# Nested Strassen for the second product of the query and key stage, in 12 groups of two heads

## The reference, cut to what matters

```
x1 = einsum('bct,bcd->bdt', x, cond_weights[idx])       # mixing of the channels, 64 x 32 x 512
q, k, v = x1 @ Wq + bq, x1 @ Wk + bk, x1 @ Wv + bv      # 2048 tokens x 512 -> 4096 (32 heads x 128)
q, k = rms_norm(q, gq), rms_norm(k, gk)                 # over all 4096 columns
out = softmax(q @ k.T / sqrt(128)) @ v                  # per head, 32 tokens of a batch with each other
x = x + out @ Wo + bo
x = x + ffn(x @ w_eff.T)                                # w_eff: weight quantised with a codebook, plus LoRA
```

## Time and profile before

| | |
|---|---|
| median of 3 runs | 1451.27 us |
| the profiled execution | 1450.27 us, of which the span of the trace 1448.4 us |
| PE busy | 1443.8 us (100% of the span) |
| DVE busy | 1079.1 us (75%) |
| POOL busy | 746.3 us (52%) |
| ACT busy | 726.7 us (50%) |
| granted clock of PE | 1.00 |

### The profile page before, as it was taken

How to read it: one execution, slowest core, us unless ns; L and a number is a source line. 1 busy time by engine, 2 the same in 40 slices (tenths; PEclk the granted TensorE clock), 3 DMA queues, 4 the chain that set the end, 5 groups by cost and what they waited for, 6 DMA issues and landing times.

```text
span 1448.4 us, 34721 instructions
## 1 busy us (share of the span) xinstructions
PE 1443.8 (100%) x14507; PEld 1200.6 (83%) x14507; DVE 1079.1 (75%) x1507; ACT 726.7 (50%) x1331; POOL 746.3 (52%) x530
## 2 busy tenths in 40 slices
PE   9999999999999999999999999999999999999999
PEld 8788888888888888888888888888888888888887
DVE  8788868687786777875478888867987667667663
ACT  7766676766766667676333333334432322222221
POOL 7668777777777877776345555514561111112100
PEclk9999999999999999999999999999999999999999
DMA  4211011110111011102443343447653334244230
GB/s 152 66 45 45 31 38 45 45 44 25 45 45 45 29 39 45 45 31 67 138 155 137 131 136 134 145 151 244 200 195 110 103 118 132 85 136 132 74 118 30
DMA packets 106989, 135.13 MB, mean 93 GB/s; under 512 B 6224, under 2 KB 89424, under 8 KB 106320
## 3 DMA queue, kind: packets, MB, share of 16 engines
q1 hardware_dynamic: 105968, 132.49, 27.7%
q10 hardware_dynamic: 864, 0.42, 0.1%
HBM read 86.75 MB, written 46.14 MB: 92 GB/s over the span
## 4 chain that ended last, share of the span: by engine, by line
PE 97%; DVE 1%; ACT 1%; DMA 0%; issue 0%; SPq 0%; DVEq 0%
PE bank L717 42%; PE bank L960 25%; PE bank L736 21%; PE bank L919 4%; PE bank L845 3%; PE bank L988 1%; PE bank L1006 1%; DMA qk<-in_x_nat 0%; PE bank L666 0%; DVE qreg L1708 0%; PE bank L1017 0%; PE bank L974 0%; ACT xs_hi L1160 0%; DVE wa L1624 0%; DVE sqst L1708 0%
## 5 line engine op out<-in xcount | busy, mean ns | idle before, releaser
L717 PE MATMUL bank<-xs_hi,wa 128*128 128x512 f32 x1792 | 563.3, 392 | 0.1
L1527 POOL TENSOR_TENSOR accr<-accr,sqst 128x512 f32<-128x512 f32 x248 | 353.2, 1435 | 147.7 <-ACT sqst L1197 107.5
L717 PEld LDWEIGHTS bank<-xs_hi,wa 128*128 128x128 f32 x1792 | 336.3, 188 | 74.1 <-DVE qk L1775 2.3
L717 PE MATMUL bank<-xs_lo,wa 128*128 128x512 f32 x896 | 348.7, 389 | 0.0
L960 PE MATMUL bank<-ot,wo_main 128*128 128x512 f32 x1344 | 316.4, 392 | 0.0
L960 PEld LDWEIGHTS bank<-ot,wo_main 128*128 128x128 f32 x1344 | 249.5, 188 | 52.6
L736 PE MATMUL bank<-wv,xs_hi 128*128 128x512 f32 (+1 forms) x1008 | 282.6, 366 | 0.1
L1624 DVE TENSOR_TENSOR wa<-wraw,wa 128x256 fp32r<-128x256 f32 (+1 forms) x160 | 157.0, 982 | 96.7 <-ACT wa L1106 95.0
L1322 ACT ACTIVATE ot<-bank,vec 128x256 fp32r<-128x256 f32 x256 | 100.3, 476 | 239.0 <-PE bank L960 146.6
L736 PEld LDWEIGHTS bank<-wv,xs_hi 128*128 128x128 f32 x1008 | 182.1, 189 | 32.9 <-issue 1.9
L717 PEld LDWEIGHTS bank<-xs_lo,wa 128*128 128x128 f32 x896 | 168.3, 188 | 33.2
(11 more groups left out here) (224 smaller groups left out, 1726.9 us busy)
## 6 DMA issues: line engine op xcount, KB each, us to landing
values_b<-v_spill SPq DMA_DIRECT2D x60, 512.0 KB, 4.9
wraw<-in_wqk SPq DMA_DIRECT2D x32, 512.0 KB, 3.5
v_spill<-qk SPq DMA_DIRECT2D x64, 256.0 KB, 2.3
v_spill<-sqst SPq DMA_DIRECT2D x64, 256.0 KB, 2.2
score_spill<-sqst SPq DMA_DIRECT2D x32, 256.0 KB, 2.0
wraw<-in_wv SPq DMA_DIRECT2D x16, 512.0 KB, 5.1
wraw<-score_spill SPq DMA_DIRECT2D x16, 512.0 KB, 4.0
spare<-in_wo SPq DMA_DIRECT2D x15, 512.0 KB, 4.8
```

The lines of the kernel that those rows point to most:

```text
L717: ins = pe.matmul(dst[:, :], wa[:, col:col + P], xpart[:, j - 1, kt, n * CH:(n + 1) * CH], start=(first and k == 0), stop=(k == 5), skip_g ...
L1527: pool.tensor_tensor(a, a, sq_slot(count), ALU.add).then_inc(acc_done, 1)
```

## The change

Second product p2 has a weight block (256 x 128) by a token block (256 x 512) for each head and half. In 12 groups of two heads (steps 12 to 59, `NEST`), the p2 of four steps are taken together as one 256 x 256 by 256 x 1024 product, and it is done by seven sub-products of Strassen-Winograd, each of one 128x128 block and 3 matmuls. These are 21 matmuls for four steps instead of 24. In a step with s % 4 = 3 PE does sub-products 1 and 2 of the next group in the place where p2(s+1) stood, then 6 and 5 (s % 4 = 0), 3 and 7 (s % 4 = 1), and 4 alone (s % 4 = 2). The other steps keep p2.

What comes with it:

- ACT copies sub-products 1, 6, 5 and 7 out of their bank (`nest_keep`), two to `rqk` in SBUF and two to bank 7, and makes the high parts x, y, z (256 columns each) and a (128); the split 1 has 256 columns instead of 512 in these steps.
- DVE makes the low parts of them, and `block_11` has two instructions in steps with s % 4 = 0 and 3, and one more, `start_11`, with s % 4 = 1. In steps 1 and 2 of a group `block_11(s)` stands in step s, not in s-1 (`late_q`), and its square and gain on ACT behind `keep_a1`.
- POOL makes the four sums of the sub-weights (`add_nest`, 128 columns each) in steps with s % 4 = 2, and once the token operands (`nest_operands`, 12 instructions in steps 4 to 10).
- The second level of the quantiser in a step moves from s % 6 = 1 to s % 4 = 0 (steps 12 to 44, nine as before).
- Bank 7 no longer takes scores; all heads' scores go to bank 3.
- SP loads 256 more columns for each group (`load_side`), saves two token blocks and the update once to HBM, and brings them back at the end.

```diff
-    return 0 if s < 6 or s > 59 else 2 if s > 6 and s % 6 == 1 else 1
+    return 0 if s < 6 or s > 59 else 2 if 12 <= s <= 44 and s % 4 == 0 else 1
...
+            def nest(s, m):
+
+                k = nest_no(s)
+                if m == 1:
+                    pe.wait_ge(nest_lo["x"], k + 1)
+                    pe.wait_ge(c11_done, s)
+                elif m == 6:
...
+                    pe.wait_ge(nest_lo["y"], k + 1)
+                    pe.wait_ge(nest_kept[1], k + 1)
+                elif m == 5:
+                    pe.wait_ge(c11_done, s + 1)
+                elif m == 3:
+                    pe.wait_ge(nest_lo["z"], k + 1)
+                    pe.wait_ge(nest_kept[5], k + 1)
+                elif m == 7:
+                    pe.wait_ge(nest_kept[6], k + 1)
+                elif m == 4:
+                    pe.wait_ge(nest_lo["a"], k + 1)
+                    pe.wait_ge(nest_kept[7], k + 1)
+                dst = bank[2 if m in (1, 6, 7, 4) else 6]
+                for i, (w_lo_part, x_lo_part) in enumerate(((0, 0), (0, 1), (1, 0))):
+                    ins = pe.matmul(dst[:, :], nest_w(m, w_lo_part), nest_x(m, x_lo_part),
+                                    start=(m in (1, 2, 5) and i == 0), stop=(i == 2), skip_group_check=True)
...
-                p2(s + 1)
+                if not nested(s + 1):
+                    p2(s + 1)
+                elif s % 4 == 3:
+                    nest(s + 1, 1)
+                    nest(s + 1, 2)
+                elif s % 4 == 0:
+                    nest(s, 6)
+                    nest(s, 5)
+                elif s % 4 == 1:
+                    nest(s - 1, 3)
+                    nest(s - 1, 7)
+                else:
+                    nest(s - 2, 4)
```

ACT's order, from `keep_a1` of a step on:

```diff
+                if late_q(s):
+                    k_upper(s)
+                    if s % 2 == 0:
+                        split_qk(1, h + 1)
                 keep_a1(s + 1)
...
+                if late_q(s):
+                    first_q(s)
+                else:
+                    k_upper(s)
+                    if s % 2 == 0 and s >= 2 and h + 1 < H:
+                        split_qk(1, h + 1)
+                if nested(s + 2) and s % 4 == 2:
+                    nest_split(s + 2, "x")
+                if nested(s + 1) and s % 4 == 3:
+                    nest_keep(s + 1, 1)
+                if nested(s) and s % 4 == 0:
+                    nest_keep(s, 6)
+                    nest_keep(s, 5)
+                if nested(s) and s % 4 == 1:
+                    nest_keep(s - 1, 7)
                 act.wait_ge(p_done[4], s + 1)
...
+                if nested(s) and s % 4 == 0:
+                    nest_split(s, "z")
+                    nest_split(s, "a")
+                if nested(s + 2) and s % 4 == 2:
+                    nest_split(s + 2, "y")
```

DVE's:

```diff
                 if s >= 2:
                     block_12(s - 1)
+                if nested(s) and s % 4 == 1:
+                    start_11(s)
...
+                if late_q(s):
+                    block_11(s)
                 if s % 2 == 1 and h + 1 < H:
                     low_qk(7, h + 1)
-                if s + 1 < N_QK:
+                if s + 1 < N_QK and not late_q(s + 1):
                     block_11(s + 1)
...
                 elif h + 1 < H:
                     low_qk(1, h + 1)
+                    if nested(s + 2) and s % 4 == 2:
+                        nest_low(s + 2, "x")
+                        nest_low(s + 2, "y")
+                    if nested(s) and s % 4 == 0:
+                        nest_low(s, "z")
+                        nest_low(s, "a")
```

and in `block_11` itself, for s % 4 = 3:

```diff
+                        dve.wait_ge(nest_kept[5], k + 1)
+                        dve.wait_ge(nest_kept[7], k + 1)
+                        link(dve.tensor_tensor(dst, bank[7][:, :], a1, ALU.add))
+                        dve.tensor_tensor(dst, dst, rqk[:, :], ALU.add).then_inc(c11_done, 1)
```

More of the change, by code:

```diff
@@ L74, with nested, late_q, nest_no @@
           4: WV_SQST + 2048, 3: WV_ACCR + 3584}
+NEST = range(3, 15)
+def nested(s):
+    return NEST[0] <= s // 4 <= NEST[-1] and s < N_QK
+def late_q(s):
+    return nested(s) and s % 4 in (1, 2)
+def nest_no(s):
+    return s // 4 - NEST[0]
 def wa_cols(j, h):
@@ L352, in build @@
         gq_hi = sem("gq_hi")
+        nest_done = {m: sem(f"n{m}_done") for m in (1, 5, 6, 7)}
+        nest_kept = {m: sem(f"n{m}_kept") for m in (1, 5, 6, 7)}
+        nest_hi = {part: sem(f"n{part}_hi") for part in "xyza"}
+        nest_lo = {part: sem(f"n{part}_lo") for part in "xyza"}
+        nest_added = sem("nest_added")
+        ld_side = sem("ld_side")
+        t_made = sem("t_made")
+        t_made_hi = sem("t_made_hi")
+        t_made_lo = sem("t_made_lo")
+        saved = sem("saved")
+        back = sem("back")
         sq_ready = sem("sq_ready")
@@ L450, in load_raw, with load_side @@
                 sp.wait_ge(s_added[4], h)
+                if nested(2 * h - 2) and h % 2 == 1:
+                    sp.wait_ge(nest_lo["x"], nest_no(2 * h) + 1)
+                    sp.wait_ge(nest_added, 4 * nest_no(2 * h) + 4)
                 sp.dma_start(wraw[:, 0:1024], wqk[h]).then_inc(ld_raw, 16)
+            def load_side(h):
+                k = nest_no(2 * h)
+                if k == 0:
+                    sp.wait_ge(saved, 48)
+                else:
+                    sp.wait_ge(nest_lo["a"], k)
+                    sp.wait_ge(nest_added, 4 * k)
+                sp.dma_start(side, wqk[h + 1][:, 256:512]).then_inc(ld_side, 16)
             load_raw(1)
@@ L485, in _ @@
                     load_raw((s + 3) // 2)
+                if s == 5:
+                    sp.wait_ge(c12_done, 5)
+                    sp.dma_start(up_spill, update[0]).then_inc(saved, 16)
+                    sp.wait_ge(x_act, x_act_at(2, 3))
+                    sp.wait_ge(x_dve, x_dve_at(2, "l3"))
+                    for part in range(2):
+                        sp.dma_start(x12_spill[part], x12[part].bitcast(F32)).then_inc(saved, 16)
+                if s % 4 == 1 and nested(s + 3):
+                    load_side((s + 3) // 2)
+                if s == 4 * NEST[-1] + 2:
+                    sp.wait_ge(p_done[2], s + 2)
+                    for part in range(2):
+                        sp.dma_start(x12[part].bitcast(F32), x12_spill[part]).then_inc(back, 16)
+                    sp.dma_start(update[0], up_spill).then_inc(back, 16)
                 if s == N_QK - 3:
@@ L759, in weights_ahead @@
             def weights_ahead(s, j):
+                if j == 7 and nested(s + 1):
+                    j = 2
+                    s += 1
                 s, j = {6: (s, 5), 5: (s + 1, 1), 1: (s - 1, 7), 7: (s + 1, 2), 2: (s - 1, 4), 4: (s, 3), 3: (s + 1, 6)}[j]
@@ L1257, in _ @@
                     keep_a3(s)
-                act.wait_ge(c11_done, s + 1)
-                square(sq_q_lo(s), 0, s % 2, blk["q_lo", s % 3], None)
-                gain("q_lo", s, gq_lo)
+                if not late_q(s):
+                    first_q(s)
                 h = s // 2
@@ new lines, in t_lo_part, with nest_operands @@
+            def t_lo_part(i, count):
+                pool.wait_ge(t_made_hi, count)
+                pool.tensor_tensor(nest_t(i, 1), spare[:, 2048 + 512 * i:2560 + 512 * i], nest_t(i, 0).bitcast(F32), ALU.subtract)\
+                    .then_inc(t_made_lo, 1)
+            def nest_operands(s):
+                r11, r12, r22, r21 = (spare[:, 512 * i:512 * (i + 1)] for i in range(4))
+                t1, t2 = spare[:, 2048:2560], spare[:, 2560:3072]
+                if s == 4:
+                    whole_x(0)
+                    whole_x(1)
+                elif s == 5:
+                    whole_t(0, r12, r11, 2)
+                    whole_x(2)
+                elif s == 6:
+                    whole_t(1, r22, t1, 4)
+                    whole_t(2, r22, r12, 4)
+                elif s == 7:
+                    whole_x(3)
+                    whole_t(3, r21, t2, 7)
+                elif s == 9:
+                    t_lo_part(1, 1)
+                    t_lo_part(0, 2)
+                elif s == 10:
+                    t_lo_part(2, 3)
+                    t_lo_part(3, 4)
@@ L1845, in _ @@
                 if s == 61:
+                    dve.wait_ge(back, 48)
                     effective(0)
```

162 lines of the change are left out of this document (149 added, 13 removed).

## The result

1510.55 us, the median of four runs (1508.47 to 1511.56), against 1451.24 before: ratio 1.0407, 95% interval 1.0389 to 1.0425. The change makes the kernel 59 us slower. The direction and the place were forecast, the size was not: 1479 was predicted, with 1506 as the end of the range.

The account below looks back on a forecast made before the run. PE was taken as the bound, busy 1443.8 of 1448.4 us. Per group -0.68 + 1.7 + 0.5 + 0.4 + 0.3 = +2.2 us, twelve groups +26.6, once +1, gave 1479 us; forecast range 1462 to 1500, whole range 1449 to 1506.

Parts of the forecast that it names:

- the ceiling of 0.68 us per group: On PE in steps with s % 4 = 2: three matmuls fewer per group save at most 0.68 us, 8.2 in all.
- p4 of B: PE's product p4 in steps with s % 4 = 3: forecast stall 1.5 to 1.8 us per group, 1.7 taken.
- the 6.2 us without POOL: On DVE: earliest start of block_12 for the s % 4 = 2 step, 6.2 us after T, if nothing holds DVE up.
- rivals 1 and 2: Whole kernel: everything hidden, 1443 us, chance 0.07; or DVE free in s % 4 = 2, 1447 to 1451 us, chance 0.20.
- p3 of B: PE's product p3 in steps with s % 4 = 3, waiting for block_22: stall 0 to 0.75 us, 0.5 taken.
- p3 of D: PE's product p3 in steps with s % 4 = 1: stall 0 to 1.1 us, 0.4 taken as mean over 12 groups.
- scores: PE's scores, waiting for a gain behind the next block_12: stall 0 to 0.9 us per group, 0.3 taken.
- The step that failed: On DVE and POOL: one of three low parts waits for POOL's addition, so block_12 starts at 7.4 to 7.7 us.
- T: Time zero of the reckoning: when the product after the scores begins on PE in a step with s % 4 = 2.
- if POOL is two squares behind: Case at the low parts on DVE: each waits a full 1.25 us and the stall at p4 is 3.4 us.
- rival 3: Saturation: POOL and DVE exclude each other and fill their shared time; +4.5 us or more per group, 1505 and up, chance 0.08.
- token operands: 12 POOL instructions in steps 4 to 10, placed in POOL's idle time: 1 us once, at most 6.

Follow-up runs that it names:

- e2: The change with POOL adding only 16 of the 512 columns of each square in steps 10 to 59; 1451.6 us, ratio 1.0001.
- e11: e8 with the 16-column additions of e2; 1447.0 us, ratio 0.9975.
- e1: The change with DVE's low parts x and y moved one step later, x behind block_12, y behind low part 7; 1495.1 us, ratio 1.0305.
- e7: e6 with block_22 ahead of low part 6 in odd steps of the groups; 1493.3 us, ratio 1.0292.
- e8: e7 with low part 4 behind the next block_12, and low part 1 ahead of the second level in steps with s % 4 = 0; 1480.6 us, ratio 1.0205.
- e6: e1 with low part 1 moved into DVE's idle time ahead of block_11; 1481.4 us, ratio 1.0216.
- e10: e8 with the nine second levels of the quantiser left out; 1470.3 us, ratio 1.0132.
- e3: The change with ten more matmuls on PE behind sub-products 1 and 2, filling the stand before p4; 1506.6 us, ratio 1.0383.

## Why the prediction was wrong in size

Right: the sign; the ceiling of 0.68 us per group (36 matmuls fewer); the place (p4 of B waits for `keep_a3`, that for `last_q`, that for `block_12(A)`, that for low parts 1, x and y held up by POOL); the 6.2 us without POOL (measured 6.15); the length of the way from `block_12(A)` to p4 of B (4.2 us, 4.3 forecast). The times of rivals 1 and 2, everything hidden or nearly so, are neared only by e2 and e11, with most of POOL's additions taken away. The rule of the Trainium skill, *SBUF — State Buffer*, "Who interferes with whom", that the two exclude each other for a whole instruction, is borne out: 1.51 us for 256 columns, of which 0.42 is the instruction.

Wrong, term by term, per group:

| term | forecast | measured |
|---|---|---|
| p4 of B | 1.7 | 2.5 (2.75 between starts less 0.23) in eleven groups, less in the last |
| p3 of B | 0.5 | 0.2 recorded, in six groups |
| p3 of D | 0.4 | 0.5 recorded, in three groups |
| scores | 0.3 | 0.8 (0.7 recorded) |
| half clock | none | 1.7 in seven groups; 0.3 net, since there p3 hardly waits |
| sum with -0.68 | +2.2 | +4.66 (45.71 - 41.05) |

**The step that failed** is "the key block's square is ready at 5.45, POOL holds till 6.75, and one of the three low parts waits for that". I let POOL be on time at T and gave it a single addition against the three low parts. In the trace POOL has been at the sums of the next head's weights and at `add_nest` and turns to the squares only at 279.77, 4.1 us after T, with two of them waiting and a third to come. So three additions lie back to back (279.77, x3), and each of the three low parts begins 1.44 us after the one before, where 0.34 is the pace in e2: every one was held up by an addition, not one of the three. `block_12(A)` is at T + 8.94 instead of 7.4 to 7.7 for that, and p4 of B starts at T + 13.17; it was due at 10.20 by the forecast and at 10.65 by PE's own pace in the trace. This is the case I had put beside it, "if POOL is two squares behind, every low part waits a full 1.25 and the stall is 3.4". I kept it for the upper end of the range and, as rival 3, for a chance of 0.08. Rival 3 has the right size (+4.5 or more per group), but saturation is not what the rows show: in the group from 366.15 to 411.86 POOL is busy for 35.7 us and DVE for 38.9 of 45.7. They are late where PE depends on them, and not busy throughout.

What is left of the sum closes nearly. Each wait of PE costs 0.16 us more than its recorded length (2.52 between starts against 2.36), and the first matmul of 512 columns after one takes 0.34 instead of 0.23. A group in which the clock stays (228.93 to 274.42, 45.5 us) has recorded waits of 2.34, 0.20, 0.52 and 0.71, and some 1.1 for the four starts: 4.9 of the 5.0 us that it lies above the 40.5 of e2. A group in which it falls (274.42 to 320.30, 45.9 us) has waits of 2.36 and 0.67, 0.5 for the two starts and 1.7 for the half clock: 5.2 of 5.4.

Once only: 1 us forecast for the token operands, at most 6. PE waited 1.71 us at 87.21 and 1.11 at 95.42, near the 12 POOL instructions, and the scores there came 3.2 us later than before; e2 and e11 have these waits too. There DVE instructions of 4 and 8 columns took 1.2 us each, where the same instruction with 16 columns took 0.19 at 91.20:

```profile
83.36 1.22 DVE L1940 TENSOR_TENSOR thr<-thr 128x4 f32<-128x4 f32 x1
84.61 1.21 DVE L1941 TENSOR_TENSOR thr<-thr 128x4 f32<-128x4 f32 x1
```

Beyond that 3.9 us of waits without a visible cause ("issue"), two of 2.5 and 0.4 in scores and one of 1.0; they stand in nearly every variant at other places, and where they come from stays open.

## What to carry to other kernels

Where PE is the bound and DVE and GpSimd both work from SBUF, add up the time that the two need the shared port for, and, while GpSimd has a backlog, count each DVE instruction with two SBUF inputs as its own time plus most of one GpSimd instruction (1.44 us here, for 0.34); saving a matmul of 0.23 us with a DVE instruction of 0.42 is a loss if that becomes 1.5. Reckon the loop from the state in which it settles, with each engine as late as the period before left it, and not from a period in which nobody was late. When such a queue is nearly full, moving one instruction out of the way of one wait shows up as the next wait (e1, e7, e8); what helped was to fill idle time of the full engine (e6, 14 us) or to take work off it (e10, 10 us) or off GpSimd (e2 and e11, which leave out what the result needs).

## What the runs showed of the hardware

- In the change PE's granted clock went to 0.50 for about 3.4 us at 7 of the 12 waits of p4, which are of 2.3 to 2.6 us but for the last (1.1), and not at the other five (230 to 270 us has 1.00 throughout). It fell at 289.9, about 1 us after PE had resumed, but elsewhere before PE had resumed (563.00 against 563.20) or 1.5 us after (151.91). In e2 it fell after a wait of 1.99 us (587.16); in e1 it stayed at 1.00 after one of 2.37 (151.63). Filled with matmuls, it never fell in 12 groups (e3). The time at half clock cost 4 us of the run, since DVE was the slower one.
- DVE and POOL took turns by single instructions: of three DVE instructions with two SBUF inputs in a row, each lasted as if it had let one addition of POOL through first (1.51, 1.51, 1.50 us, against 0.42 with short additions).
- The smallest DVE instructions are held up as the others are: 4 columns took 1.22 us and 256 took 1.51, both beside POOL instructions of 1.28 us or more.
- An instruction of the level with one tile as its input (L2017) is held up too: 1.79 us in e1 at 280.49, 0.80 free.
